# Gated delta rule in a decoder layer: query norms from VectorE block transposes and moves inside SBUF, in place of TensorE transposes

## What is computed

```python
mixed = silu(causal_conv1d(hidden @ w_qkv, conv_w))          # 16 q and k heads, 32 v heads, of 128
q = q * rsqrt(sum(q * q, axis=-1) + 1e-6)                    # l2 norm of queries, and of keys
k = k * rsqrt(sum(k * k, axis=-1) + 1e-6)
beta, g = sigmoid(hidden @ w_b), -exp(A_log) * softplus(hidden @ w_a + dt_bias)

def step(St, inp):                                           # one token of one head
    q_t, k_t, v_t, g_t, b_t = inp
    St = St * exp(g_t)
    delta = (v_t - k_t @ St) * b_t
    St = St + outer(k_t, delta)
    return St, (q_t * 128 ** -0.5) @ St

core = core * rsqrt(mean(core * core, axis=-1) + 1e-6) * norm_weight * silu(hidden @ w_z)
out = core @ w_out
```

## Time and profile before

| | us |
|---|---|
| median of 3 runs | 3355.97 (3355.91 to 3357.96) |
| the profiled execution | 3361.55 |
| its span in the trace | 3359.8 |

### The profile page before, as it was taken

The page is one execution under the profiler, slowest core; times in us unless marked ns, Lnnn a source line. Parts: engine busy times, 40 slices in busy tenths (PEclk is TensorE's granted clock), DMA queues, the critical chain, the costliest instruction groups (busy, mean ns, idle before and its releaser), DMA issues. The chain is left out here.

```text
span 3359.8 us, 58642 instructions
## 1 busy us (share of the span) xinstructions
PE 3261.2 (97%) x20832; PEld 2280.0 (68%) x20832; DVE 2452.5 (73%) x3622; ACT 1541.5 (46%) x4983; POOL 1864.0 (55%) x1824
## 2 busy tenths in 40 slices
PE   5899999999999999999999999999989999999999
PEld 2577777777777777777777777777766777764444
DVE  6799999999999999999999999999940111024553
ACT  2456555655565556555655565556532000011232
POOL 2677677777777777677767777777740000011132
PEclk8999999999999999999999999999989999999999
DMA  3123222322223222322232222222215222211001
GB/s 100 42 61 76 76 64 58 73 73 64 63 72 77 62 64 65 79 61 63 71 79 66 57 70 74 66 61 69 87 51 210 75 100 91 84 38 63 0 13 38
DMA packets 132287, 231.75 MB, mean 69 GB/s; under 512 B 15872, under 2 KB 81536, under 8 KB 126464
## 3 DMA queue, kind: packets, MB, share of 16 engines
q1 hardware_dynamic: 130704, 220.92, 23.8%
q10 hardware_dynamic: 1296, 7.08, 0.5%
HBM read 156.39 MB, written 71.57 MB: 68 GB/s over the span
## 5 line engine op out<-in xcount | busy, mean ns | idle before, releaser
L718 PE MATMUL acc<-xT,wc 128*128 128x512 f32 x2048 | 937.9, 601 | 2.8 <-PEq L110 2.0
L718 PEld LDWEIGHTS acc<-xT,wc 128*128 128x128 f32 x2048 | 370.9, 191 | 374.7 <-issue 374.1
L1003 DVE SCALAR_TENSOR_TENSOR d_conv<-acc,wc,d_conv 128x511 f32<-128x511 f32 (+2 forms) x768 | 566.5, 738 | 43.2 <-ACT d_conv L1172 34.0
L731 PE MATMUL acc<-wc,xT 128*128 128x256 f32 x2048 | 473.4, 384 | 0.0
L731 PEld LDWEIGHTS acc<-wc,xT 128*128 128x128 f32 x2048 | 379.1, 190 | 46.2
L620 POOL TENSOR_TENSOR d_bf<-d_kks,d_gam 128x512 f32<-128x512 f32 x128 | 160.2, 1273 | 344.3 <-ACT d_kks L1218 344.3
L1522 PE MATMUL acc<-t_area 128*128 128x512 f32 x768 | 334.6, 595 | 1.0 <-ACT t_area L1971 1.0
L1031 DVE STREAM_TRANSPOSE d_em<-d_dm 128x1024 f16<-128x1024 f16 x256 | 314.5, 1228 | 2.2
L2028 POOL TENSOR_SCALAR t_veps<-t_mv 128x1 f32<-128x1 f32 x32 | 9.7, 303 | 544.4 <-DVE t_mv L1767 544.4
L1522 PEld LDWEIGHTS acc<-t_area 128*128 128x128 f32 x768 | 239.3, 314 | 86.6 <-issue 1.6
L1038 DVE TENSOR_TENSOR d_zm<-d_tz,cons 128x512 f16<-128x512 f32 x384 | 258.9, 674 | 52.4 <-PE d_tz L786 47.5
(11 more groups left out here) (227 smaller groups left out, 7171.5 us busy)
## 6 DMA issues: line engine op xcount, KB each, us to landing
d_decay<-decay_rows SPq DMA_DIRECT2D x64, 512.0 KB, 5.6
v_rows<-d_vb SPq DMA_DIRECT2D x256, 128.0 KB, 2.3
d_vn<-v_rows SPq DMA_DIRECT2D x64, 512.0 KB, 3.6
core_rows<-d_ob SPq DMA_DIRECT2D x256, 128.0 KB, 2.2
t_area<-core_rows SPq DMA_DIRECT2D x30, 1024.0 KB, 4.8
wc<-in_w SPq DMA_DIRECT2D x96, 256.0 KB, 2.9
t_x<-in_x SPq DMA_DIRECT2D x4, 1024.0 KB, 9.5
t_area<-in_wout ACTq DMA_DIRECT2D x2, 2048.0 KB, 13.2
```

The source lines that it names most:

```text
L718: last = nc.tensor.matmul(bank(TILE[j])[:, :], wtile(j, k), xT[:, k, r % B * S:(r % B + 1) * S], start=k == 0, stop=k == KT - 1)
L731: last = nc.tensor.matmul(bank(f"z{j}")[:, i * GV * P:(i + 1) * GV * P].rearrange("p (h n) -> p h n", h=GV), xT[:, k, r % B * S + (2 * j + ...
L1003: nc.vector.scalar_tensor_tensor(c[:, d:S], bank(TILE[j])[:, 0:S - d], tap(j, KS - 1 - d), c[:, d:S], ALU.mult, ALU.add).then_inc(taps, 1)
```

## The change

`q_turn`, its place in the ring of PSUM banks and its semaphore go. In their place VectorE turns the 32x32 blocks of `qT` into a new buffer `qf` (`flip_q`, behind `flip_v`), SP moves the 16 groups of blocks to their places in a new buffer `qn` (`move_q`, 16 transfers of 32 partitions x 512 bytes inside SBUF, between `load_v` and `store_o`), and ScalarE squares `qn` over itself. With NC = 4, the count for all moves of a unit is MOVED = 256. The squares of the keys now write over `kraw`, in f32, where they wrote bf16 to `junk`, and the waits that kept the two users of `junk` apart go; a wait of `silu` for `k_squares` is new, for the next keys in `kraw`.

```diff
             def store_v(m):
-                sp.wait_ge(v_flipped, count(m))
+                sp.wait_ge(v_flipped, at(m, 2, 1))
...
+            def move_q(m):
+                sp.wait_ge(v_flipped, at(m, 2, 2))
+                wait(sp, q_squares, at(back(m, 1), NC, NC))
+                for a in range(NC):
+                    for b in range(NC):
+                        sp.dma_start(qn[b * 32:(b + 1) * 32, a].rearrange("p c j -> p (c j)"),
+                                     qf[a * 32:(a + 1) * 32, b].rearrange("p c j -> p (c j)")).then_inc(q_moved, 16)
...
-            def q_turn(n):
-                pe.wait_ge(silued, nth(n, "silued", 1))
-                ring_free(n, "q_turn")
-                turn(bank("q_turn"), qT[third(n)], q_turned)
...
+            def flip_q(m):
+                dve.wait_ge(silued, nth(m, "silued", 1))
+                wait(dve, q_moved, at(back(m, 1), MOVED, MOVED))
+                nc.vector.transpose(qf[:, :, :, :], qT[third(m)][:, :].rearrange("p (c b j) -> p b c j", c=NC, b=NC)).then_inc(v_flipped, 1)
...
                 if j == 0:
                     wait(act, k_turned, count(n, 1))
+                    wait(act, k_squares, at(back(n, 1), NC, NC))
...
-            def squares(src, spare, dst, sem_, scale=1.0):
+            def squares(src, out, dst, sem_, scale=1.0):
                 for c in range(NC):
-                    nc.scalar.activation(junk[:, spare + c, :], chunk(src, c), ACT.Square, scale=scale,
-                                         accum_out=dst[:, c:c + 1]).then_inc(sem_, 1)
+                    nc.scalar.activation(out(c), src(c), ACT.Square, scale=scale, accum_out=dst[:, c:c + 1]).then_inc(sem_, 1)
...
-                wait(act, q_squares, at(back(n, 2), NC, NC))
-                squares(bank("k_turn"), 0, kss, k_squares)
+                squares(lambda c: chunk(bank("k_turn"), c), lambda c: chunk(kraw, c), kss, k_squares)
...
-                act.wait_ge(q_turned, count(n))
+                act.wait_ge(q_moved, at(n, MOVED, MOVED))
                 wait(act, eq_ready, count(n, 1))
-                wait(act, k_squares, min(at(back(n, -1), NC, NC), NC * ITERS))
-                squares(bank("q_turn"), 0, qss, q_squares, scale=(RMS_EPS * HD) ** 0.5)
+                squares(lambda c: qn[:, :, c, :], lambda c: qn[:, :, c, :], qss, q_squares, scale=(RMS_EPS * HD) ** 0.5)
```

## The result

The changed kernel takes 3368.84 us in the median of 6 runs (3368.00 to 3374.27), against 3356.00 for the kernel before in the same session: 1.004 of it, 95% interval [1.003, 1.005]. In a second session it took 3366.83 us, 1.0029 [1.0017, 1.0040]. It is slower by some 10 to 13 us, where 14.5 us less was forecast, and the time lies above the stated range.

What follows compares the result with a forecast made beforehand. TensorE was taken as the bound, with VectorE setting the pace at one place. 0.23 us a slot over 63 slots, the additions hidden, gave 3355.97 - 14.5 = 3341.5 us; 8-in-10 range 3328 to 3361, chance 0.52.

Steps and rivals of the forecast that it cites:

- The gain on TensorE: Removing four TensorE transposes (0.47 us a slot) was to save 0.23 us a slot, 14.5 us over 63 slots.
- The two late hand-overs: On TensorE, `grow` (L868) waiting for `uu` loses 0.08 us; `read_k` (L839) waiting for `state` loses 0.15.
- Rival 1: All the TensorE saving arrives: 0.39 to 0.47 us a slot, -25 to -30 us, 3326 to 3331; chance 0.14.
- `flip_q`: The added VectorE block transpose takes 0.6 us, wholly inside VectorE's idle gap of 0.71 us, and costs nothing.
- The keys' squares over `kraw`: Squares of `khat` on ScalarE, written in f32: at most 0.05 us each, 0.2 in all, with no effect.
- The price of an issue: Each of SP's sixteen moves takes 0.44 us to issue, with 2.3 us to landing after the last.
- Who waits for the squares: `solved(s, 2)` behind them on ScalarE; the moves stay hidden, landing 2.6 us before the squares must start.
- the prediction's own formula: With x us per issue on SP, ScalarE's squares end 16x + 2.3 + 1.2 us after 1006.55; limit 1019.7.
- Rival 2: Late moves hold ScalarE's squares ahead of `solved(s, 2)`: at 0.7 us an issue +107 us, 3463; chance 0.15.
- Rival 3: VectorE's `flip_q` or block writes disturb the chain by some 0.2 us, cancelling the gain: 3356, no change; chance 0.19.
- `d_uu` came after the squares with no idle time: Sign on ScalarE that the forecast is wrong; no size given.
- Its other sign, a later `flip_o`: Sign of a wrong forecast: `flip_o` on VectorE starting more than 4.96 us after the z projection.

Runs made afterwards that it cites:

- the slowest experiment: The changed kernel with the squares of q moved to the end of ScalarE's list and `q_norm` at its old place: 3638.88 us, 1.084 of before.

## Why the prediction was wrong

- **The gain on TensorE: right, a little small.** 0.23 us a slot was the sum; the kernel without moves shows 37.22 - 36.94 = 0.28. The two late hand-overs (L868 and L839 of before) are there: TensorE's starts in the changed slot leave 0.09 us more for `grow` and 0.10 more for `level_d(3)`, and `read_k` starts 0.06 us after `state` (its weight load names no wait, though one had been expected). 63 x 0.28 = 17.6 us, and 17 were measured. Rival 1, 0.39 to 0.47 us, is out.
- **`flip_q`: right.** 0.60 us taken, 0.60 measured, in the gap of 0.71.
- **The keys' squares over `kraw`: right.** The kernel without moves has this edit too, and it has all of the gain.
- **The price of an issue: the first step that failed, a mis-sized term.** It was taken from `store_v` at 0.44 us (median), with its 817 ns as the far end. It is 0.59 for the instruction and 0.63 from one start to the next. Sixteen make 10.67 us and not 7. The measured value lies inside the stated bounds, but the middle row was taken over from another form: 32 partitions, one row of 512 bytes each, from SBUF to SBUF is not 32 partitions, four rows of 1 KB each, from SBUF to DRAM. Landing was 1.8 us, not 2.3. With four moves, 2.42 us on SP, nothing waits and the gain is there, although `q_norm` stands where it stood.
- **Who waits for the squares: the second step that failed.** The prediction followed ScalarE's queue to `solved(s, 2)` and gave the squares until 1019.7. `q_norm` on GpSimd was never priced. In the trace of before GpSimd reaches it at 1018.83, so from squares that end later than about 1018.9 its queue is held up. By the prediction's own formula that begins at (1018.9 - 1006.55 - 3.5) / 16 = 0.55 us each, and in slots with a late `load_v` at 0.47, where it had 0.60 and 0.52. At 0.63 all slots are past it. VectorE's 0.8 us to spare take up the first of it. ScalarE's way, by contrast, was only at its limit in the slot shown: the squares end 1022.08 - 1008.83 = 13.25 us after `load_v`, where 1019.7 - 1006.55 = 13.15 were allowed. With `q_norm` out of the way 20 to 22 us came back.
- **Rival 2** had the place and the sign (late transfers, the squares' wait), with 0.15 of the chances. Its price, by its formula at 0.63 us, is 0.4 us a slot and 1.7 in late ones, +40 us in all; measured were 10 to 13. It came by the queue of GpSimd for the most part, where some of the lateness is absorbed. Rival 3, VectorE, is out.
- **The ends of the stage.** The sum multiplies one slot by 63. The third slot and the drain, where less work hides a wait, each lost 4 to 5 us at once against the kernel without the moves.
- The prediction said that it would be wrong if ScalarE's `d_uu` came after the squares with no idle time. It does so in the slot shown (1021.99), but this is a sign of the lateness and not its price. Its other sign, a later `flip_o`, did not come: 1011.12 - 1006.16 = 4.96 us, as before.

The Trainium skill's rule that speaks for TensorE in 128x128 transposes ("VectorE: DVE Perf Modes", section "Rules for kernel authors") does not decide this case: with the same block transposes on VectorE the kernel is 0.4% slower or 0.5% faster than with TensorE's, by how the blocks are moved.

## What to carry over

When a result becomes late, list every engine that waits for it, the small operations too: an addition of 128x4 that nobody needs for a slot stopped GpSimd's queue, and cost more than the wait that was being watched. A wait that the profile names on TensorE need not cost anything: compare the starts of the groups, and look at the slots at the ends of the stage too. Where work is put in an in-order queue at a place that was right for an early result, it has to be moved when the result comes later. Count transfers and not only bytes: five transfers by way of DRAM instead of sixteen turned a loss of 0.3 to 0.4% into a gain of 0.5%, and so did four, which put the blocks in wrong places.

## What the runs showed of the hardware

- SP's issues differ by their form, in the median: `load_v`, 128 rows from DRAM, 0.34 us; `store_v`, 32 partitions to DRAM, 0.44; the moves, 32 partitions from SBUF to SBUF, 0.58 to 0.59, with 512 or 2048 bytes a row alike.
- Of a GpSimd operation and VectorE's scan (`d_gam`) that meet, the second to start takes longer. In 2000 us of the changed trace a `pT` takes 1.27 us alone (20 of them) and 1.28 when it started ahead of the scan (35), but 2.19 when it started during the scan (51). The scan takes 1.21 us with no GpSimd operation running at its start (13 in the trace of before) and 2.09 with one (90). The Trainium skill ("SBUF — State Buffer", section "SBUF: two separate sides") has a port pair that VectorE, with two SBUF inputs, and GpSimd hold one at a time, whichever starts first; these durations agree. It bears on this case: in the changed slot the two `pT`, now later, take 3.42 us and L615 2.08, where they took 2.49 and 1.16, which uses up the 0.81 us that GpSimd had been idle behind `q_norm` before.
- The granted clock fell after TensorE had waited. In the drain of the changed kernel it waits 4.84 us, and from 2491.00 to 2495.70 us, with TensorE busy again, the clock is 0.50, the lower of its two levels; from 2495.70 it is 1.00. In the slowest experiment, where slots are 5 us longer, it was 0.957 over the span, against 0.991 in the changed kernel, and 0.95 against 1.00 from 900 to 1300 us.
- A small load issued close behind large ones of its queue lands later: the taps, 8 KB, landed 2.7 us after their issue in the median with everything pushed together, 1.7 in the kernel without moves, and ScalarE's wait for them was 5.6 us and not 4.6.
